# Scores of both head halves on four 32-row groups at once, in the short-key attention of layers 0 and 2

## The reference, cut to what matters

```python
qh, kh, vh = proj(q), proj(k), proj(v)              # 16 heads, 16 dimensions each
scores = einsum('bhqd,bhkd->bhqk', qh, kh) / 4      # 77 keys
scores = where(mask == 0, -1e9, scores)             # layer 0 only
attn = softmax(scores)
ctx = einsum('bhqk,bhkd->bhqd', attn, vh)
return concat(ctx) @ Wo.T + bo
```

## Time and profile before

| what | us |
|---|---|
| time, three runs | 2664.62, 2665.01, 2671.63; median 2665.01 |
| span of the profiled execution, first to last instruction | 2662.1 |
| TensorE (PE) busy in it | 2421.0 |
| first to last score matmul of layer 0 | 30.5 to 230.3 |
| first to last score matmul of layer 2 | 1712.0 to 1934.1 |

### The profile page before, as it was taken

One profiled execution on the slowest core, in us unless ns is written; L12 is line 12 of the kernel. 1 busy time (PEld: TensorE's weight loads), 2 busy tenths in 40 slices (PEclk: granted clock), 3 DMA queues, 4 the chain that ended last, 5 costly groups with the idle time before them and its releaser, 6 DMA issues. The chain is left out here.

```text
span 2662.1 us, 42263 instructions
## 1 busy us (share of the span) xinstructions
PE 2421.0 (91%) x12786; PEld 1426.1 (54%) x12787; DVE 1610.9 (61%) x3274; ACT 1294.8 (49%) x2567; POOL 1310.4 (49%) x2112
## 2 busy tenths in 40 slices
PE   6997999999996996899999999899969975999997
PEld 3554666766663563344444453455546663666664
DVE  5885664755554985777868777488866654122221
ACT  4664443534443794566666667566643421222221
POOL 3665664134445662233443535467875215666663
PEclk9998999999998998999999999899989977999998
DMA  4001000000000005131231311010004151222222
GB/s 139 6 1 63 5 0 0 1 1 1 23 26 16 1 1 127 31 78 49 67 84 38 86 57 56 25 32 17 1 16 152 48 200 29 44 46 46 45 46 28
DMA packets 86176, 115.24 MB, mean 43 GB/s; under 512 B 15624, under 2 KB 65584, under 8 KB 84320
## 3 DMA queue, kind: packets, MB, share of 16 engines
q1 hardware_dynamic: 67456, 92.55, 11.5%
q0 software_dynamic: 18528, 20.31, 4.7%
HBM read 77.92 MB, written 34.64 MB: 42 GB/s over the span
## 5 line engine op out<-in xcount | busy, mean ns | idle before, releaser
L3452 ACT ACTIVATE L2S_pT<-L2S_t_ps 128x512 f32<-128x512 f32 (+3 forms) x768 | 356.4, 491 | 220.7 <-PE L2S_t_ps L3273 211.9
L3516 DVE TENSOR_REDUCE L2S_mx<-L2S_s_ps 128x1 f32<-128x768 f32 (+7 forms) x384 | 350.0, 950 | 105.8 <-PE L2S_s_ps L3196 105.0
L3273 PE MATMUL L2S_t_ps<-L2S_q,L2S_k 98*128 98x512 bf16 (+3 forms) x768 | 249.2, 335 | 17.5 <-DMA L2S_q<-L2S_mrow 6.8
L3758 POOL TENSOR_SCALAR_AFFINE_SELECT L2S_pT<-L2S_pT 128x128 f32<-128x128 f32 x512 | 151.7, 311 | 174.8 <-ACT L2S_pT L3452 170.4
L3195 PE MATMUL L2S_s_ps<-L2S_k,L2S_q 96*128 96x512 bf16 (+3 forms) x768 | 199.2, 332 | 11.8 <-DVE L2S_mx L3516 8.3
L622 POOL TENSOR_TENSOR L_prob<-L_prob,L_rc 128x616 f32<-128x616 f32 x64 | 82.3, 1287 | 231.3 <-DVE L_rc L555 231.3
L4134 DVE TENSOR_TENSOR L3B_h<-L3B_si,L3B_u_ps 128x512 f32<-128x512 f32 x71 | 48.8, 687 | 237.2 <-PE L3B_u_ps L4077 218.9
L4051 POOL DMA_INDIRECT out<-L3B_y,L3F_rows x71 | 114.8, 1616 | 132.4 <-DVE L3B_y L4140 120.1
L3273 PEld LDWEIGHTS L2S_t_ps<-L2S_q,L2S_k 98*128 98x128 bf16 x768 | 73.1, 98 | 196.6 <-ACT L2S_pT L3452 127.8
L3373 PE MATMUL L2S_o_ps<-L2S_pT,L2S_v 128*32 128x512 f32 (+3 forms) x1536 | 165.4, 504 | 0.0
L319 PE MATMUL L_scores<-weights,L_xT 128*128 128x308 f32 x512 | 143.1, 423 | 2.2 <-ACT L_xT L442 1.6
(11 more groups left out here) (549 smaller groups left out, 5770.7 us busy)
## 6 DMA issues: line engine op xcount, KB each, us to landing
qk_parts<-L2S_part SPq DMA_DIRECT2D x84, 128.0 KB, 2.4
L2S_q<-qk_parts SPq DMA_DIRECT2D x32, 192.0 KB, 3.3
L2S_k<-qk_parts SPq DMA_DIRECT2D x30, 192.0 KB, 3.3
L2S_q<-qk_parts SPq DMA_DIRECT2D x32, 128.0 KB, 3.1
L3F_w<-in_L_gu SPq DMA_DIRECT2D x8, 512.0 KB, 7.6
weights<-in_L_w SPq DMA_DIRECT2D x8, 512.0 KB, 9.3
out<-x_sb SPq DMA_DIRECT2D x8, 512.0 KB, 4.0
expert_rows<-L_xn SPq DMA_DIRECT2D x8, 512.0 KB, 3.5
```

What stands on the lines that cost most here:

```text
L3273: nc.tensor.matmul(o[:, lo:512], k6[:, q % 2, j, kt * P:(kt + 1) * P], q6[:, q % 2, c, j, lo:512], start=True, stop=True).then_inc(s["t_fu ...
L3452: nc.scalar.activation(pT[:, st % SLOTS, j, lo:512], t_ps[j % 2][:, lo:512], ACT.Exp, scale=SK).then_inc(s["exp_done"], 1)
L3516: nc.vector.tensor_reduce(dst, src, AX.X, ALU.max).then_inc(s["mx_done"], 1)
L3758: nc.gpsimd.affine_select(out=edge, in_=edge, compare_op=ALU.is_ge, fill=0.0, base=0, pattern=[[1, P]], channel_multiplier=-1).then_inc(s[ ...
```

## The change

The two score tiles of two banks each become one tile `S_ps` of four banks. Scores are made for two units at a time (both halves of a tile of tokens): in each bank `j` stand the scores of heads 2j and 2j+1 of both halves, 154 columns for each half. For each half there are four float32 matmuls with a contraction of 32 rows on the row groups 0, 32, 64 and 96, each to its own bank, in place of two of 64 rows and 308 columns. In layer 0 four mask matmuls of 308 columns precede them, as many for a pair of units as before.

`scores(U)` now waits until the whole pair before it has been read (`shifted >= U`), and `s_full` is raised by 2 at the end. All four engines go in steps of two units; the order of pieces is new, and differs between the two streams and by `u`. The distance of `turn` to `scores` is 2 units rather than 3. In layer 0 `query(.., 1)` moves to `u` = 3, the gathers from 3 and 4 to 2 and 4, and the last `combine` of a group to `u` = 1 of the next; in layer 2 `query(.., 1)` and the second `forward` move to 3 and the first gather to 2. Sizes of `prob`, `probT`, `T_ps` and `R_ps` are unchanged.

```diff
-        S_ps = [ctx.enter_context(nc.psum_tensor(f"L0_scores{i}", [P, 2, 512], F32)) for i in range(2)]
+        S_ps = ctx.enter_context(nc.psum_tensor("L0_scores", [P, ROW_GROUPS, 512], F32))   # 4; WIDE = 2 * NC = 154
...
+        def ring_uses(g, u):
+            uses = []
+            if u == 1 and 2 <= g <= G + 1:
+                uses += [("c", g - 2, 3)]
+            if g + 1 < G:
+                uses += {0: [("x", g + 1, dh) for dh in range(KD)], 1: [("q", g + 1, 0)], 3: [("q", g + 1, 1)]}.get(u, [])
+            if 1 <= g <= G:
+                uses += {2: [("o", g - 1, 0)], 4: [("o", g - 1, 1)], 5: [("c", g - 1, 0)], 6: [("c", g - 1, 1)], 7: [("c", g - 1, 2)]}.get(u, [])
+            if u == 7 and g % 2 == 0 and g // 2 + 1 < B:
+                uses += [("v", g // 2 + 1)]
+            return uses
...  TensorE, layer 0
-                pe.wait_ge(shifted, U + 1)
-                for a in range(2):
-                    nc.tensor.matmul(S_ps[U % 2][:, a, 0:BK], identb[:], wide(maskb...), start=True, stop=False)
-                for a in range(2):
-                    mm = nc.tensor.matmul(S_ps[U % 2][:, a, 0:BK], qT[64 * a:64 * a + 64, g % 2, hf, i * P:(i + 1) * P],
-                                          kblk[64 * a:64 * a + 64, b % 2, hf, :, :]..., start=False, stop=True)
-                mm.then_inc(s_full, 1)
+                if U:
+                    pe.wait_ge(shifted, U)
+                for j in range(ROW_GROUPS):
+                    nc.tensor.matmul(S_ps[:, j, 0:2 * WIDE], identb[:], wide(maskb...), start=True, stop=False, skip_group_check=True)
+                for hf in range(2):
+                    for j in range(ROW_GROUPS):
+                        mm = nc.tensor.matmul(S_ps[:, j, hf * WIDE:(hf + 1) * WIDE], qT[32 * j:32 * j + 32, g % 2, hf, i * P:(i + 1) * P],
+                                              kblk[32 * j:32 * j + 32, b % 2, hf, 2 * (j % 2):2 * (j % 2) + 2, :]..., start=False, stop=True, skip_group_check=True)
+                mm.then_inc(s_full, 2)
...
-            for s in range(UNITS + UN):     # scores(s), ring pieces of u, turn(s - LAG), LAG = 3
+            for s in range(0, STEPS, 2):
                 g, u = divmod(s, UN)
+                first = ring_uses(g, u)
                 if s < UNITS:
                     scores(s)
+                if u in (2, 4):
+                    for use in first:
+                        piece[use[0]](*use[1:])
+                if 0 <= s - 2 < UNITS:
+                    turn(s - 2)
+                if u not in (2, 4):
+                    for use in first:
+                        piece[use[0]](*use[1:])
+                if 0 <= s - 2 < UNITS:
+                    turn(s - 1)
+                for use in ring_uses(g, u + 1):
+                    piece[use[0]](*use[1:])
...  ScalarE, layer 0
+            for s in range(0, STEPS, 2):
+                if u in (2, 4):
+                    if s < UNITS:
+                        exp(s)
+                    for use in first:
+                        piece[use[0]](*use[1:])
+                    if 0 <= s - 2 < UNITS:
+                        turn(s - 2)
+                else:
+                    if 0 <= s - 2 < UNITS:
+                        turn(s - 2)
+                    for use in first[:1]:
+                        piece[use[0]](*use[1:])
+                    if s < UNITS:
+                        exp(s)
+                    for use in first[1:]:
+                        piece[use[0]](*use[1:])
+                if 0 <= s - 2 < UNITS:
+                    turn(s - 1)
+                if s < UNITS:
+                    exp(s + 1)
+                for use in ring_uses(g, u + 1):
+                    piece[use[0]](*use[1:])
+                # then the normalise calls of u and u + 1
...  VectorE
+            for s in range(0, UNITS, 2):
+                g, u = divmod(s, UN)
+                unit(s)
+                unit(s + 1)
+                others(g, u)
+                total(s)
+                others(g, u + 1)
+                total(s + 1)
...  GpSimd
-                if 0 <= s - 2 < UNITS:
+                if s % 2 == 0 and 0 <= s - 2 < UNITS:
                     divide(s - 2)
+                    divide(s - 1)
```

More of the change, by code:

```diff
@@ L819, in combine @@
                 mm.then_inc(ring_full, 1)
+            piece = {"x": turn_x, "q": query, "o": gather, "c": combine, "v": values}
             pe.wait_ge(identb_done, 1)
@@ L910, in _ @@
             query(0, 1)
-            for s in range(UNITS + UN):
+            for s in range(0, STEPS, 2):
                 g, u = divmod(s, UN)
-                if 0 <= s - 2 < UNITS:
[L914 to L932, removed]
-                    normalise(g + 2, u - 3)
-                if 0 <= s - LAG < UNITS:
-                    turn(s - LAG)
+                first = ring_uses(g, u)
+                if u in (2, 4):
[14 more added lines that the diff above has]
+                        piece[use[0]](*use[1:])
+                if 0 <= s - 2 < UNITS:
+                    turn(s - 1)
[3 more added lines that the diff above has]
+                    piece[use[0]](*use[1:])
+                for v in (u, u + 1):
+                    if g + 2 < G and 3 <= v <= 6:
+                        normalise(g + 2, v - 3)
         @block.vector
@@ L987, in _, with others @@
             blocks(0)
-            dve.sem_inc(shifted, 2)
             nc.vector.memset(T_ps[96:P, (KCH - 1) * P:KCH * P], 0.0).then_inc(t_free, 1)
             masks(0)
-            for s in range(UNITS + 1):
-                g, u = divmod(s, UN)
-                if s < UNITS:
-                    unit(s)
-                if s >= 1:
-                    total(s - 1)
+            def others(g, u):
                 if g + 2 < G:
@@ L1550, in _, with others @@
             ins.then_inc(bias_done, 1)
-            for s in range(LAST):
-                g, u = divmod(s, UN)
-                if s < UNITS:
-                    unit(s)
-                if 1 <= s <= UNITS:
-                    total(s - 1)
+            def others(g, u):
                 if (g, u) in ((0, 6), (0, 7)):
@@ L1574, in _ @@
                     update(G - 1, (3, 5, 6, 7).index(u))
+            for s in range(0, LAST, 2):
+                g, u = divmod(s, UN)
+                if s < UNITS:
+                    unit(s)
+                    unit(s + 1)
+                others(g, u)
+                if s < UNITS:
+                    total(s)
+                others(g, u + 1)
+                if s < UNITS:
+                    total(s + 1)
         @block.gpsimd
```

164 lines of the change are left out of this document (87 added, 77 removed).

## The result

| | median | runs | profiled span |
|---|---|---|---|
| before | 2666.85 us | 4, 2664.62 to 2671.63 | 2662.1 us |
| after | 2697.14 us | 4, 2691.73 to 2702.07 | 2690.0 us |

The ratio is 1.011, interval 1.0097 to 1.0126: 30 us slower, where 6 us faster was predicted, and outside the range given. Layer 0 costs 8.0 us of the 28 by which the span grew (layer 1's first product starts at 451.6 instead of 443.6 us), layer 2 20.3 (from its first score product to layer 3's first product 298.1 instead of 277.8).

What follows compares the result with a forecast made beforehand. TensorE was taken as the bound in both stages, VectorE close behind. Passes and changes -59, gather stalls +38, late starts +15 gave -6 us: span 2656, median 2659 us; own range 2645 to 2671, whole range with rivals 2628 to 2690.

Steps and rivals of the forecast that it cites:

- Passes: TensorE's score products, both stages: four row groups side by side, 0.52 us of passes, saving 0.92 us for each pair.
- The rival of two at a time: Score products: row groups run only two at a time, 33 us over the forecast, 2692 us; chance 0.11.
- Stalls behind ScalarE's copy: TensorE before turn(s-1) at u = 2 and 4: waits 1.22 us (layer 2: 1.15) for the copy; 38 us in all.
- The walk of layer 0's middle groups: Pair-by-pair schedule of an odd and an even group of layer 0: together 52.9 us against 53.06 before.
- Layer 2: the same walk gives ... 59.3: Pair-by-pair schedule of two groups of layer 2: 59.3 us against 59.86; layer 2 in all -4 us.
- The first groups, counted at nothing: First group of each stage: the forecast's sum has no separate term for it.
- Last groups: Last group of each stage gets shorter: some 1.5 us in layer 0, 4 us credited in layer 2.
- every pair goes at the gather pair's pace: Rival: VectorE's lateness is carried on, u = 0 and 6 take 7.3 us too; 22 us slower, 2687; chance 0.12.
- -59 for the passes: TensorE's score passes and tiling changes: 0.92 us saved in each of 64 pairs, 59 us in all.
- +38 for the stalls: Pairs with a gather, u = 2 and 4: stalls of 1.2 us, twice in each of 16 groups, 38 us.
- +15 for late starts in the other pairs: Pairs other than those with the gather stalls, both stages: late starts add 15 us.
- The signs named beforehand: Passes 0.13 us apart, 1.2 us idle before turn(s-1), PE busy some 87%, 64 units of layer 0 in about 200 us.

Runs made afterwards that it cites:

- e4_two_wide: Kernel after, its order kept, with the earlier score products (two of 64 rows and 308 columns for each half): 2711.5 us, 1.0164 of before.
- e10_two_wide_again: e7_all with the earlier score products, two of 64 rows and 308 columns for each half: 2659.4 us, 0.9967 of before.
- e1_turn_first: Kernel after, at u = 2 and 4 the gather between the turns, turn(s-2) copied before exp(s) and the gather's copy: 2660.6 us, 0.9977 of before.
- e11_join_at_4: Kernel after, with layer 2's join of tile 1 at u = 4, behind that pair's units, instead of u = 3: 2685.3 us, 1.0066 of before.
- e7_all: e1_turn_first plus both copies of x ahead of exp(s) at u = 0, and both turns one unit later: 2640.4 us, 0.9903 of before.
- e2_join_last: Kernel after, in layer 2 at u = 2 VectorE's join of the second tile behind total(s+1): 2692.0 us, 1.0100 of before.

## Why the prediction was wrong, step by step

- **Passes: right.** 0.92 us a pair rested on 0.72 for the products with their changes; 0.74 measured. The rival of two at a time falls: run by itself (`e4_two_wide`, `e10_two_wide_again`) it costs 14 to 19 us more, not its 33.
- **Stalls behind ScalarE's copy: right in place and sign; that 38 and 36.5 agree is in part luck.** 1.22 forecast, 1.54 and 1.21 measured in layer 0; in layer 2 1.15 forecast, 1.12 at u = 2 and 2.46 at u = 4. The waits sum to 50.9 us where 38 was put. `e1_turn_first` gives back 36.5, but in that are also slow-clock stretches and the join's lateness of layer 2, which the 38 did not count.
- **The walk of layer 0's middle groups: right within 2%.** 52.9 for two groups, 53.76 measured, odd group first: u = 2 was 7.8 and 7.5 (forecast 7.98 and 7.58), u = 4 6.6 (6.43), u = 6 4.9 and 6.7 (5.16 and 6.2), u = 0 6.4 and 7.2 (6.1 and 6.96). But the forecast had these two groups 0.2 us shorter than before, and they are 0.7 longer.
- **"Layer 2: the same walk gives ... 59.3": the step that failed.** 66.7 was measured. "The same walk" carried over layer 0's order and left out one instruction of VectorE: `join` of tile 1 at u = 3, which stands ahead of `total(s+1)` and waits for a product that this pair makes last. Before, it never waited; now 12.1 us in 143. VectorE's lateness, which the prediction carried only to the next pair, then went on: late exp, late copy, idle PE. Of the 7.4 us by which two groups missed, the two pairs at u = 4 are 4.7 (9.41 + 11.09 against 2 x 7.9), and 1.7 of that (11.09 less 9.41) is the clock, with two combines of 1.92 and 1.67 rather than 1.03. `e11_join_at_4`, which moves the join alone, brings the two groups to 62.4 us; 4.3 of the 7.4 are back. `e1_turn_first`, which leaves the join and moves the turns, brings them to 59.5. So the loss takes both: a late VectorE, and a copy queued behind exp that passes the lateness on. What the odd groups' u = 0 costs beyond its forecast (10.76 against 9.0) was not tested by itself; the same pair in the next odd group takes 9.75 at a clock of 1.00, where this one has 0.84.
- **The first groups, counted at nothing.** They cost 4.65 us in layer 0 and 5.4 in layer 2, a third of the result. There are no gathers or combines yet to fill a pair, which is argued and not tested. The clock is part of it: 0.94 and 0.87, where before had 1.00. With all three orders mended (`e7_all`) the first group of layer 0 takes 22.1 us again, as before. A timeline of the kernel after shows it: PE waits 1.97 us for the copy of x that stands behind exp, and then the query product takes 3.62 us, most of it at the 1.2 GHz level, where it took 1.99 before.

```profile
34.49 0.58 ACT L877 ACTIVATE L_xT<-L_ring 128x512 f32<-128x512 f32 x1
...
35.13 3.62 PE L781 MATMUL L_ring<-L_xT,weights 128*128 128x512 f32 x4 [1.97 <-ACT L_xT L877]
```

- **Last groups: over-credited in layer 2.** 1.6 and 1.5 us shorter (forecast 1.5 and 4). That layer 0 agrees may be luck: in `e2_join_last` and `e11_join_at_4`, the same code there, its pair at u = 4 takes 1.6 us more at a clock of 0.81, and nothing is gained on before.
- **The rivals.** The one nearest in time had 0.12: "every pair goes at the gather pair's pace", 2687. Its condition, VectorE over 1 us late at u = 2, came true only in the last group of layer 2 (1.9 us, against a start that waits for nothing but the products). In layer 0 VectorE was at most 0.4 us late there, and in groups 4 to 7 of layer 2 not at all: it stood waiting for the products. Nor did u = 0 and 6 of layer 0 go at 7.3. What the rival had right is that VectorE's lateness costs time; but the place was u = 4 of layer 2, 1.4 us late in each of groups 4 to 7, and the cause the join, which it doesn't name. That its 2687 is nearest is luck. VectorE's timeline of the kernel after, the start of a pair at u = 2 in layer 2:

```profile
1848.09 0.80 DVE L1508 TENSOR_REDUCE L_mx<-L_scores 128x8 f32<-128x616 f32 x1 [0.91 <-PE L_scores L1275]
```

- **The terms of the sum.** -59 for the passes rests on products that measured as forecast. +38 for the stalls was 51 of waiting. So that the span can grow by 28, the last term, +15 for late starts in the other pairs, must be about +36, an estimate by difference. No row had priced the 15 by itself, either: it is what the walk left over.
- **The signs named beforehand nearly all came, and the time still fell outside the range.** Passes 0.13 us apart, the idle before `turn(s-1)`, PE at 88%; only the 64 units of layer 0 took 205 rather than 200 us. None of them asked what is particular to layer 2, where most of the loss was.

The sum as measured, by group: layer 0 +0.9 before its first score product, first group +4.65, the other seven +0.9, +1.6 from its last score product to layer 1; layer 2's first group +5.4, groups 2 to 7 +16.7, the last -1.5, and -0.3 behind it. Groups 2 to 7 of layer 2 had been forecast at about 0. Parts of this change from trace to trace: in `e2_join_last` and `e11_join_at_4`, with the same code in layer 0, layer 1 starts 10.9 and 9.1 us later than before, not 8.0.

What remains open: the 0.9 and 1.6 us at the two ends of layer 0, and how much of layer 2's loss is the clock alone, which no experiment held still. Rows at both levels give a size: in groups 4 to 7, two pairs at u = 4 take 11.09 us and two 9.41, and u = 0 takes 10.76 and 9.75, the longer ones always at a clock of 0.84 or 0.85 and the shorter at 1.00. That is some 4.4 of the 16.7 us, an estimate.

## What to carry to other kernels

A change that merges two steps into one saves on the engine it was made for, and takes slack from every in-order queue: before trusting the sum, list for each engine each instruction that now waits for something the same merged step makes last, and what is queued behind it, in every stage and in its first round too. Copies that hand a single tile back must stand ahead of work that waits for a slower engine. Single repairs can measure as nothing until the others are in place (the copies of x: 0 alone, 9 us together), so try the combination before giving one up. And before a filler is credited with holding the clock up, look whether the slow stretch moves by itself between traces of the same code.

## What the runs showed of the hardware

- Four row groups of 32 rows ran fully side by side: sixteen float32 instructions of 154 columns in 0.74 us with the change of tiling, in fours 0.13 us apart.
- The clock fell in the middle of stages: in a group with PE busy 18.10 of 26.77 us, its longest idle 2.50 us, the granted clock was 0.94, and in one with 20.76 of 27.17 us, its longest idle 4.63, it was 0.87. At the 1.2 GHz level the same product took 1.92 instead of 1.03 us and `values` 4.37 instead of 2.34.
- The same instructions met the slow stretch at different places in different runs: the first group of layer 0 took 26.8, 29.0 and 28.0 us in three traces of the same code (granted 0.94, 0.82, 0.88).
- The length of one idle didn't decide. The pair at u = 4 of the group before has the same wait of 2.46 us, and its combines run at the 2.4 GHz level; two rows of TensorE's timeline of the kernel after:

```profile
1828.78 0.74 PE L1284 MATMUL L_turned<-ident,L_prob 128*128 128x128 f32 x5 [2.46 <-ACT L_probT L1422]
...
1829.46 1.03 PE L1309 MATMUL L_ring<-weights,L_oT 128*128 128x256 f32 x4
```

That pair takes 9.41 us, the one at 1855.07 with slow combines 11.09. What tells the two apart was not found. In `e11_join_at_4` and `e1_turn_first`, where these waits are shorter or gone, all four such pairs have a clock of 1.00.
